# Conditioned residual layer on one core: loads split over two hardware queues by SBUF halves, and six product tiles copied out of PSUM ahead of their bias

## What is computed

```python
# x: (4, 1024, 512) float32; cond: (4, 256); W: (1536, 512); b: (512,)
x_mean = jnp.mean(x, axis=1, keepdims=True)
hidden = jnp.concatenate([cond, cond], axis=-1)
fused = jnp.concatenate([x, x_mean * ones_L, hidden[:, None, :] * ones_L], axis=-1)
out = x + jax.nn.relu(jnp.einsum('bld,do->blo', fused, W) + b)
```

## Time and profile before

| what | value |
|---|---|
| median of 3 runs | 114.31 us (114.14 to 115.6) |
| the profiled execution | 114.67 us, of which the profile's span is 112.9 us |
| busy, share of the span | PE 99.7 us (88%), DVE 82.9 (73%), ACT 48.2 (43%), POOL 46.0 (41%) |
| loads and stores | 20.08 MB, 178 GB/s on the mean |

### The profile page before, as it was taken

The page is one execution under the profiler, slowest core; times in us unless marked ns, Lnnn a source line. Parts: engine busy times, 40 slices in busy tenths (PEclk is TensorE's granted clock), DMA queues, the critical chain, the costliest instruction groups (busy, mean ns, idle before and its releaser), DMA issues.

```text
span 112.9 us, 1832 instructions
## 1 busy us (share of the span) xinstructions
PE 99.7 (88%) x526; PEld 79.9 (71%) x526; DVE 82.9 (73%) x148; ACT 48.2 (43%) x118; POOL 46.0 (41%) x43
## 2 busy tenths in 40 slices
PE   5959999841999899999999999999999999999900
PEld 2319998521788588677888886888888868999900
DVE  1027849890278899999999992899999976797530
ACT  4148415910029985028738400595654006433310
POOL 5348400008000000099985620446666089980000
PEclk9999999998599999999999999999999999999995
DMA  2999999999999999994869539100391670687966
GB/s 82 259 239 231 218 203 237 339 261 219 221 219 218 223 219 222 219 217 84 198 178 226 144 76 253 43 0 0 76 252 43 160 211 6 136 234 179 255 142 171
DMA packets 36023, 20.08 MB, mean 178 GB/s; under 512 B 1968, under 2 KB 34864, under 8 KB 36016
## 3 DMA queue, kind: packets, MB, share of 16 engines
q1 hardware_dynamic: 34576, 18.69, 77.1%
q10 hardware_dynamic: 1248, 0.79, 2.6%
q0 software_dynamic: 192, 0.52, 1.8%
HBM read 11.60 MB, written 8.39 MB: 177 GB/s over the span
## 4 chain that ended last, share of the span: by engine, by line
PE 60%; SPq 17%; DMA 8%; ACT 5%; DVE 3%; issue 3%; DVEq 0%
PE ps_y L406 60%; DMA xa<-in_x_dram 8%; SPq L162 8%; ACT relu_t L256 3%; SPq L141 3%; SPq L171 2%; ACT xh L236 2%; SPq L175 1%; DVE ps_xt L300 1%; PE ps_mean L425 1%; SPq L169 1%; SPq L146 1%; SPq L173 1%; DVE back L317 0%; DVE xa L342 0%
## 5 line engine op out<-in xcount | busy, mean ns | idle before, releaser
L406 PE MATMUL ps_y<-xh,w1h 128*128 128x256 f32 (+2 forms) x160 | 52.9, 355 | 2.5 <-ACT xh L236 1.4
L406 PE MATMUL ps_y<-xl,w1h 128*128 128x256 f32 (+2 forms) x160 | 51.8, 348 | 0.0
L207 POOL TENSOR_TENSOR xa<-xa,back 128x512 f32 x28 | 35.7, 1303 | 37.5 <-DVE back L317 37.5
L406 PE MATMUL ps_y<-xh,w1l 128*128 (+2 forms) x144 | 50.5, 368 | 0.0
L406 PEld LDWEIGHTS ps_y<-xh,w1h 128*128 128x128 f32 x160 | 28.8, 191 | 9.2 <-issue 2.4
L256 ACT ACTIVATE relu_t<-ps_y,bias 128x512 f32<-128x512 f32 (+1 forms) x32 | 20.0, 633 | 31.2 <-DVE bias L349 22.0
L300 DVE STREAM_TRANSPOSE ps_xt<-xa 128x512 f32<-128x512 f32 (+1 forms) x36 | 22.2, 640 | 12.9 <-DMA xa<-in_x_dram 12.6
L406 PEld LDWEIGHTS ps_y<-xl,w1h 128*128 128x128 f32 x160 | 28.8, 191 | 3.6
L406 PEld LDWEIGHTS ps_y<-xh,w1l 128*128 128x128 f32 x144 | 27.2, 190 | 4.5
L236 ACT ACTIVATE xh<-ps_xt 128x512 fp32r<-128x512 f32 (+1 forms) x36 | 19.7, 548 | 23.3 <-DVE ps_xt L300 23.2
L306 DVE TENSOR_TENSOR xl<-ps_xt,xh 128x512 fp32r<-128x512 f32 (+1 forms) x36 | 22.3, 618 | 4.4 <-ACT xh L236 4.4
(11 more groups left out here) (21 smaller groups left out, 19.5 us busy)
## 6 DMA issues: line engine op xcount, KB each, us to landing
xa<-in_x_dram SPq DMA_DIRECT2D x28, 256.0 KB, 6.7
out_dram<-xa SPq DMA_DIRECT2D x28, 256.0 KB, 3.5
xa<-in_x_dram SPq DMA_DIRECT2D x8, 128.0 KB, 5.9
w<-in_L_cond_W_dram SPq DMA_DIRECT2D x4, 256.0 KB, 6.8
w<-in_L_cond_W_dram SPq DMA_DIRECT2D x2, 512.0 KB, 9.7
w<-in_L_cond_W_dram POOLq DMA_DIRECT2D x4, 128.0 KB, 4.6
out_dram<-xa SPq DMA_DIRECT2D x4, 128.0 KB, 2.8
out_dram<-xa ACTq DMA_DIRECT2D x4, 128.0 KB, 2.4
```

The costliest lines, as they stand in the source:

```text
L207: nc.gpsimd.tensor_tensor(rows, rows, back[:, t], ALU.add).then_inc(added, 1)
L406: return nc.tensor.matmul(ps_y[:, t, ls], lhs, rhs, start=start, stop=stop, skip_group_check=True)
```

## The change

**Loads.** SP now issues only quadrants 0 and 1 of everything that is cut by quadrant, ACT quadrants 2 and 3; the upper half of group 1 is issued by POOL, behind its second W1 subtraction. W1's loads are cut by slice: k=0, k=1, and k=2 and 3 together. W3 now stands ahead of the condition and of W2. Groups 2 to 7 are issued by SP without a wait between them, the upper halves by ACT at fixed places in its stream.

**Tiles copied out.** `SAVED` = 6: tiles 0 and 1 of group 1 are copied out of PSUM too, so PE's first two tiles of group 2 wait for a copy, not for a relu. The constant part and `mean_bias(0)` stand behind tile 1 of group 1 instead of tile 0.

**Orders.** Group 0's low W1 products follow each slice. The relus and the pieces of groups 2 and 3 alternate one to one; the first piece of group 2 stands behind `sum_bias(0)`. 12 warm-up matmuls instead of 14. PE's loop is turned by a group, with the same work in the same order.

```diff
-WARM = 14
+WARM = 12
+SAVED = 6
+    added_by = [NK * H if g < H else NK * (g + 1) for g in range(LAST)]
...
 @block.sync
-            load_x0(sp, 0)
-            load_w1(sp, 1, range(0, 2), w1_landed)
-            load_x0(sp, 1)
-            load_x(1, 1)
-            sp.dma_start(cond_c[:], cv).then_inc(cond_landed, 16)
-            for j in ORDER:
-                sp.dma_start(w2[Q * j:Q * j + Q], wv[1, j]).then_inc(w2_landed, 16)
+            load_x0(sp, 0, LOW)
+            load_w1(sp, 0, 1, LOW)
+            load_w1(sp, 1, 2, LOW)
+            load_w1(sp, 2, NK, LOW)
+            load_x0(sp, 1, LOW)
+            load_x(sp, 1, LOW)
             for r in range(2):
                 sp.dma_start(w3[:, r], w3v[r]).then_inc(w3_landed, 16)
+            sp.dma_start(cond_c[:], cv).then_inc(cond_landed, 16)
+            load_w2(sp, LOW)
...
-            load_x(2, 0)
-            with sp.Fori(1, B - 1) as b:
-                sp.wait_ge(x_landed[1], 16 * NQ * b)
-                load_x(H * b + 1, 1)
...
+            for g in range(2, G):
+                load_x(sp, g, LOW)
 @block.gpsimd
-            load_w1(pool, 0, range(2, NQ), w1_q23_landed)
-            load_w1(pool, 1, range(2, NQ), w1_q23_landed)
...
+                if k == 1:
+                    for j in HIGH:
+                        pool.dma_start(xa[Q * j:Q * j + Q, 1], xv[1, j]).then_inc(x1_q23_landed, 16)
 @block.scalar
-            load_w1(act, 0, range(0, 2), w1_landed)
+            load_x0(act, 0, HIGH)
             act.wait_ge(ones_set, 1)
             nc.scalar.activation(act_warm[:], ones[:, 0:1], ACT.Relu)
+            load_w1(act, 0, 1, HIGH)
+            load_w1(act, 1, 2, HIGH)
+            load_w1(act, 2, NK, HIGH)
+            load_x0(act, 1, HIGH)
...
-                if g == 0:
+                if n < SAVED:
                     act.wait_ge(y_saved, n + 1)
...
+            for k in range(NK):
                 w1_high(k)
                 x_high(k)
-            x_beside = (1, 0, 1, 1, 0, 2, 1, 1)
...
+            load_w2(act, HIGH)
+            n_x = pieces_to(H)
             for n in range(NK, n_x):
-                if n == pieces_to(H) - 1:
+                if n == n_x - 1:
                     save(0)
-                if n == n_x - 1:
-                    for t in range(1, NK):
-                        save(t)
                 x_high(n)
+                if n == n_x - 3:
+                    load_x(act, 2, HIGH)
+            for n in range(1, SAVED):
+                save(n)
+            load_x(act, 3, HIGH)
             for n in range(len(tiles)):
-                for _n in range(x_beside[n] if n < H * NK else 0):
+                relu(n)
+                for _n in range(1 if n < H * NK else 0):
                     x_high(n_x)
                     n_x += 1
-                relu(n)
+                if n in (1, 3, 5, 7):
+                    load_x(act, SLOTS + n // 2, HIGH)
```

More of the change, by code:

```diff
@@ L28 @@
 ORDER = (0, 2, 1, 3)
+LOW, HIGH = (0, 1), (2, 3)
 NL = 512
@@ L341, in residual @@
                 rows = xa[:, g, l // Q:(l + nl) // Q, Q * t:Q * t + Q]
-                nc.vector.tensor_tensor(rows, rows, back[:, t, 0:nl // Q], ALU.add).then_inc(last_added, 1)
+                nc.vector.tensor_tensor(rows, rows, back[:, n % BACK_RING, 0:nl // Q], ALU.add).then_inc(last_added, 1)
             def sum_bias(b):
@@ L395, in _ @@
                     n_x += 1
-                if g + SLOTS - 1 < G and g > 0 and g % H == 0 and t == NK - 1:
-                    mean_terms(g // H + 1)
+                if g + SLOTS - 1 < G and n // NK > 0 and n // NK % H == 0 and n % NK == NK - 1:
+                    mean_terms(n // NK // H + 1)
         @block.tensor
@@ L426, in mean_bias, with group0_low @@
                 last.then_inc(mean_done, 1)
+            def group0_low(half, k):
+                ls = slice(half * HL, (half + 1) * HL)
+                if half == 0:
+                    pe.wait_ge(w1l_ready, k + 1)
+                for t in range(NK):
+                    last = mm(t, ls, w1l[:, k, t], xh[:, 0, k, ls], stop=(half == 1 and k == NK - 1))
+                    if half == 1 and k == NK - 1:
+                        last.then_inc(y_ready, 1)
             for half in range(2):
@@ L440, in _ @@
                         mm(t, ls, w1h[:, k, t], xl[:, 0, k, ls])
-            for t in range(NK):
-                for k in range(NK):
-                    if t == 0:
-                        pe.wait_ge(w1l_ready, k + 1)
-                    last = mm(t, slice(0, NL), w1l[:, k, t], xh[:, 0, k], stop=(k == NK - 1))
-                last.then_inc(y_ready, 1)
+                    if half == 0 and k > 0:
+                        group0_low(half, k - 1)
+                    elif half == 1:
+                        group0_low(half, k)
+                if half == 0:
+                    group0_low(half, NK - 1)
             for t in range(NK):
@@ L460, in _ @@
                     mean_bias(0)
-            def even_group(b):
-                for t in range(NK):
-                    pe.wait_ge(relu_done, NK * (H * b - 1) + t + 1)
-                    tile(H * b, (H * b) % SLOTS, t)
-                    if t == 2:
-                        pe.wait_ge(bias_ready, b)
-                        mean_bias(b)
+            for t in range(NK):
+                if NK + t < SAVED:
+                    pe.wait_ge(y_saved, NK + t + 1)
+                else:
+                    pe.wait_ge(relu_done, NK + t + 1)
+                tile(H, H % SLOTS, t)
+                if t == 2:
+                    pe.wait_ge(bias_ready, 1)
+                    mean_bias(1)
             with pe.Fori(1, B - 1) as b:
-                even_group(b)
                 for t in range(NK):
@@ L474, in _ @@
                     tile(H * b + 1, (H * b + 1) % SLOTS, t)
-            even_group(B - 1)
+                for t in range(NK):
+                    pe.wait_ge(relu_done, NK * (H * b + 1) + t + 1)
+                    tile(H * b + H, (H * b + H) % SLOTS, t)
+                    if t == 2:
+                        pe.wait_ge(bias_ready, b + 1)
+                        mean_bias(b + 1)
             for n, (g, l, nl, t) in enumerate(tiles):
```

88 lines of the change are left out of this document (40 added, 48 removed).

## The result

The changed kernel is slower: a median of 120.98 us (118.96 to 121.71, 4 runs) beside 114.66 us for the kernel before on the same chip, a ratio of 1.043 (95% interval 1.026 to 1.059). The forecast was 110.4, the range ended at 114.6, and slower had 0.12: wrong in size and in sign. The profiled execution took 121.58 us, its span is 119.8. In several kernels single runs were some per cent longer than the rest, here the profiled one too; the ratios leave those out, the medians and ranges don't, so the ratio puts the loss at 4.9 us and the profile at 6.9. Lines have moved: `mm` is L409, `turn_x` L307, `save` L249, ACT's loads of x L150, POOL's load of group 1 L204, `mean_terms` L336 to L341, `mean_bias` L428, `sum_bias` L353 and L356.

What follows compares the result with a forecast made beforehand. The end was taken to hang on DVE's time of bias 0, and this on the loads. Bias 0 6.1 us earlier, less 2.0 given back, wins 4.1: profiled 114.67 to 110.6, forecast 110.4, range 109.2 to 114.6.

Steps and rivals of the forecast that it cites:

- Everything above needs x of group 1 by about 17 us: Load deadlines for the earlier first bias: x of group 1 by 17 us, W2 by 22, group 2 by 27.
- I take 300, between them: Load rate with two queues on two halves: 300 GB/s assumed, between 220 and 401, so loads land in time.
- Rival 4: POOL's two issues of group 1's x take longer or get little rate; 2 us more gives 112.4; chance 0.09.
- as nothing paces it: SP's queue, full from 7 us on without waits between groups; named in rival 3 on ACT's issue time.
- rival 2: Load rate stays at 220 to 233 GB/s, W2 and group 2 land late, 2.8 us lost: 113.0; chance 0.22.
- Rival 1: PE's clock falls in the 2.5 us wait before `mean_bias(1)`, costing 1.6 us: 111.7; chance 0.08.
- 0.3 hidden: Of the 1.6 us half-clock cost behind the wait before `mean_bias(1)`, 0.3 lies under DVE's 4.0 us.
- Rival 3: ACT is held by its own load issues between relus, 5.5 us more: 115.9; chance 0.15.
- Rival 5: The reordering does nothing for the end because PE is the bound anyway; no chance of its own given.
- The chain of 4.0 us from the end of `mean_terms(1)` to group 3: Turn-backs, bias 1 and a relu put group 3's start 4.0 us after `mean_terms(1)` ends: 42.9 to 46.9.
- The shifted stretch from group 3 to the end: PE's matmuls from group 3 on are only shifted; from there to the end 61.9 us, as before.
- One more piece: One more DVE piece stands behind bias 0, giving back 1.43 us of the gain.

Runs made afterwards that it cites:

- x1_act: Changed kernel with group 1's upper half issued by ACT behind its second copy of W1, not by POOL; 119.71 us, ratio 1.048.
- x1_sp: Changed kernel with group 1 whole on SP again, ahead of W3; 114.51 us, ratio 0.996.
- its three children: `x1_sp` with group 3's upper half one copy earlier on ACT, SP paced from group 4, or both; 113.01, 112.19, 112.65 us.
- old_loads: Changed kernel with the loads of the kernel before (queues, cuts, pacing), keeping new orders and six copies; 112.69 us, ratio 0.990.
- old_loads_w3first: `old_loads` with W3 loaded ahead of the condition and W2; 112.21 us, ratio 0.985.
- x1_sp_paced: `x1_sp` with SP waiting, before group 4 and each later one, for the group two before; 112.19 us, ratio 0.977.
- the best kernels: Apparently `x1_sp_paced`, the same with group 3 earlier on ACT, and two with ACT issuing group 1's half at the start; ratios 0.977, 0.975, 0.982, 0.972.

## Why the prediction was wrong

**The step that failed** is "Everything above needs x of group 1 by about 17 us", answered with "I take 300, between them" and "in time". The landing was worked out as bytes over a rate for all queues together. It is a matter of when a DMA is issued and of what the other queues hold at that moment: POOL's half, issued at 9.1 and 9.9, moved its first packet at 15.0, with most of W3 ahead of it, and came at 22.0. Rival 4 had the mechanism, "Each microsecond beyond 17 of group 1's landing ... shifts everything", but laid it on POOL's issues (which took 0.72 each) and put 2 us on it and 0.09. It was 5, and `x1_act` shows that it wasn't POOL's doing.

**The size.** The end of the chain's 19.34 us (three tiles into group 4) was forecast at 46.9 + 19.34 = 66.2 and came at 77.2, 11.0 late, as the execution was (121.6 for 110.6). Group 1 began 6.0 late. Bias 0 came 8.5 late, 2.5 more, of which 2.2 is two tiles that ran for a good part at half clock (26.27 to 33.99, 7.7 us for 5.5). `mean_terms(1)` came 10.1 late, 1.6 more, from the wait for group 3 less what DVE won back. The clock behind `mean_bias(1)` took the last 0.9.

**A wait that I hadn't listed.** I gave a date to groups 1 and 2 and none to group 3. Its upper half stands behind ACT's sixth copy, at 34.1 with everything late and at 26.2 in `x1_sp`, and lands some 10 us later behind SP's unpaced lower halves. `x1_sp` against its three children puts its price at 1.0 to 2.4 us, with the clock that fell behind it. I had priced "as nothing paces it" for ACT's issue time alone.

**The rate, rival 2.** From 9 to 34 us it was 229, 227 and 202 (9 to 14, 14 to 22, 22 to 34), at or below what rival 2 said, but the 113.0 worked out for it is far off, and the rate isn't what decides: `x1_sp`, on the same two queues, had 261 GB/s from 3 to 20 us, not much over the 247 of the changed kernel, and took 114.5. The Trainium skill, "SBUF — State Buffer", section "Can I just issue two DMAs to hit both halves?", holds two such DMAs to be 6% faster than one. By the rows, 290 for 202 with both queues full is 44% more, which speaks against it. The 210 behind a backlog says nothing of it, as one queue alone moved then.

The Trainium skill, "DMA: Bandwidth & Descriptors", section "Queues, rings and completion order", has each DMA engine take turns between the queues that have work, a packet at a time. The trace agrees from the first packet on: near-equal counts of packets (22, 27 and 29; 167 and 156), and 6 us from 15.0 to the last one at 21.1, where a third of 220 GB/s gives 7 for POOL's 0.5 MB. It doesn't agree before that: with turns from the issue on, the half would have landed near 17, but its queue got no turn until 15.0.

**Rival 1** happened beside the rest: PE waited 2.50 us before `mean_bias(1)`, the clock was 0.70 from 55 to 60, and the 96 matmuls took 1.6 us more, the price that I had given. My "0.3 hidden" was too little, 0.7 was. **Rival 3** did for one pair: most of ACT's issues took 0.3 to 0.5 us, as in the row of 0.86 for two, but the two at 40.0 took 1.0 and 1.2, and ACT stood idle for 1.62 us behind them. It cost nothing here, as DVE waited for group 3's x until 44.36. **Rival 5** is refuted by `old_loads`.

**What was right.** The chain of 4.0 us from the end of `mean_terms(1)` to group 3, in `old_loads`, `old_loads_w3first` and `x1_sp_paced` (43.48 to 47.52) alike. The shifted stretch from group 3 to the end, 61.9 us here too (57.93 to 119.8). "One more piece" and the pieces' pace (1.4). Group 0 ended at 19.7, for 19.9, in part by luck: three of ACT's issues ran beside its table load (1.76 to 3.11) and not behind it, so PE began 1.0 sooner, and group 0 took 0.8 longer than worked out. The gain of the orders is smaller than forecast: by the ratios 1.1 and 1.8 us in `old_loads` and its twin, 2.1 to 3.2 in the best kernels, for 4.1, since W3 or W2 comes no sooner and bias 0 stands at 28.6 to 30.4 in all but one of their profiles, not at 27.2 (in `x1_sp_paced` DVE waits until 24.41 for W2, where "W2 by 22" was asked).

**Open.** Why a queue gets no turn in the first microseconds behind other queues' work: the packets show that it is so, not by what. It is open too what moves group 1's landing by 2 to 3 us between two runs of the same loads (16.5 and 18.85, 15.68 and 18.75). Not tried: ACT's early loads held back too.
